# Label slots, first w7 loads, scaled tiles and early label rows moved in a one-core recommender kernel

## The reference, cut to what matters

```python
x: (1024, 50, 300)   label_embedding: (1024, 200, 300)      # all float32
q1 = attn_pool(x, mask, w1, b1, w2)      # softmax over 50 rows of exp((x @ w1 + b1) @ w2),
q2 = attn_pool(x, mask, w3, b3, w4)      # then the weighted sum of the rows
h = concat([q1, q2], axis=1) @ w5 + b5                      # (1024, 300)
f6 = h @ w6 + b6
iu, ju = triu_indices(300, k=1)                             # 44850 pairs
cross = h[:, iu] * h[:, ju] * (v @ v.T)[iu, ju]
f7 = cross @ w7 + b7                                        # (1024, 44850) @ (44850, 300)
out8 = concat([f6, f7], axis=1) @ w8 + b8                   # (1024, 300)
return einsum('bu,bku->bk', out8, label_embedding)          # (1024, 200)
```

## Time and profile before

| | |
|---|---|
| median of 3 runs | 1762.22 us (1760.65 to 1764.42) |
| time of the profiled execution | 1760.75 us |
| its span, first to last instruction | 1758.9 us |
| granted TensorE clock, mean | 0.968 |
| TensorE busy | 1583.0 us, 90% |
| VectorE busy | 1421.1 us, 81% |
| ScalarE busy | 996.4 us, 57% |
| DMA moved | 615.20 MB, mean 350 GB/s |

### The profile page before, as it was taken

The page is one execution under the profiler, slowest core; times in us unless marked ns, Lnnn a source line. Parts: engine busy times, 40 slices in busy tenths (PEclk is TensorE's granted clock), DMA queues, the critical chain, the costliest instruction groups (busy, mean ns, idle before and its releaser), DMA issues.

```text
span 1758.9 us, 25341 instructions
## 1 busy us (share of the span) xinstructions
PE 1583.0 (90%) x7086; PEld 1159.8 (66%) x7086; DVE 1421.1 (81%) x5487; ACT 996.4 (57%) x2931; POOL 137.9 (8%) x96
## 2 busy tenths in 40 slices
PE   2889999999999999999999999899999999998700
PEld 1467677677777777777777777577777777765400
DVE  8897888873898999799998986567777668678956
ACT  7665777764565646464655644344444444433497
POOL 5000000000000000000000000000000000003366
PEclk9999999999999999999999999899999999999955
DMA  7799877977899999999999899999999989999898
GB/s 295 268 390 369 288 273 242 330 279 258 299 332 388 364 409 354 413 357 370 392 359 395 324 393 383 413 358 328 359 381 374 334 314 406 350 357 406 329 397 361
DMA packets 170385, 615.20 MB, mean 350 GB/s; under 512 B 20784, under 2 KB 49421, under 8 KB 162053
## 3 DMA queue, kind: packets, MB, share of 16 engines
q1 hardware_dynamic: 106469, 368.44, 55.0%
q10 hardware_dynamic: 61696, 242.33, 37.0%
q0 software_dynamic: 2080, 2.81, 0.5%
HBM read 609.70 MB, written 3.79 MB: 349 GB/s over the span
## 4 chain that ended last, share of the span: by engine, by line
PE 66%; DMA 15%; DVE 11%; ACT 4%; issue 2%; POOL 1%; SPq 1%; ACTq 0%; DVEq 0%; POOLq 0%
PE bank L706 59%; DMA wring<-in_w7p 8%; DVE stream L1074 5%; DVE cring L1053 3%; DMA stream<-in_x 3%; PE bank L656 3%; DVE junk L953 2%; DMA stream<-in_label 2%; ACT stream L873 2%; PE bank L671 2%; DMA sring<-hrows 1%; ACT wring L862 1%; ACT stage L873 1%; PE bank L684 1%; ACT absjunk L771 1%
## 5 line engine op out<-in xcount | busy, mean ns | idle before, releaser
L706 PE MATMUL bank<-wring,cring 128*128 128x300 f32 (+1 forms) x5616 | 1445.3, 419 | 42.3 <-ACT wring L862 17.3
L706 PEld LDWEIGHTS bank<-wring,cring 128*128 128x128 f32 (+1 forms) x5616 | 1064.6, 191 | 407.2 <-issue 33.5
L862 ACT ACTIVATE wring<-wring,gcol 128x300 f32<-128x300 f32 x1403 | 655.4, 534 | 673.4 <-PE bank L706 579.9
L1053 DVE TENSOR_TENSOR cring<-lefts,sring 128x1024 f32<-128x1024 f32 (+2 forms) x312 | 372.5, 1194 | 190.5 <-PE bank L706 162.2
L1074 DVE SCALAR_TENSOR_TENSOR stream<-stream,out 128x300 f32<-128x300 f32 x1080 | 442.2, 469 | 0.0
L953 DVE SCALAR_TENSOR_TENSOR junk<-stream,ubc 128x300 bf16<-128x300 f32 x784 | 320.5, 469 | 28.3 <-DMA stream<-in_x 28.3
L771 ACT ACTIVATE absjunk<-stream 128x300 bf16<-128x300 f32 x448 | 196.0, 439 | 12.5 <-DMA stream<-in_x 7.1
L1074 DVE DVE_READ_ACCUMULATOR stream<-stream,out 128x1 f32 x1080 | 92.2, 85 | 0.0
L771 ACT ACTIVATION_READ_ACCUMULATOR absjunk<-stream 128x1 f32 x448 | 83.9, 187 | 0.0
L1074 DVE SCALAR_TENSOR_TENSOR stream<-stream,bank 128x300 f32<-128x300 f32 x160 | 64.8, 460 | 22.2 <-DMA stream<-in_label 22.2
L607 POOL DMA_DIRECT2D scores<-score x6 | 3.4, 570 | 987.8 <-DVE stream L1074 829.2
(11 more groups left out here) (94 smaller groups left out, 510.0 us busy)
## 6 DMA issues: line engine op xcount, KB each, us to landing
wring<-in_w7p ACTq DMA_DIRECT2D x365, 600.0 KB, 7.5
stream<-in_label SPq DMA_DIRECT2D x276, 750.0 KB, 10.4
stream<-in_x SPq DMA_DIRECT2D x64, 1050.0 KB, 12.6
sring<-hrows SPq DMA_DIRECT2D x152, 256.0 KB
stage<-in_label SPq DMA_DIRECT2D x44, 750.0 KB, 7.7
wring<-in_w7p ACTq DMA_DIRECT2D x18, 450.0 KB, 5.2
wring<-in_w7p ACTq DMA_DIRECT2D x18, 300.0 KB, 6.5
sring<-hrows SPq DMA_DIRECT2D x96, 44.0 KB
```

The source lines that it names most:

```text
L706: mm = pe.matmul(acc[b % 4][:, 0:E], cring[0:rows, p % CSLOTS, b % 2, j0 + j, :], w, start=(p == BEGIN[b] and j == 0), stop=(p == END[b] - ...
L862: ins = nc.scalar.activation(w, w, ACT.Copy, scale=gcol[:, t:t + 1])
L1053: nc.vector.tensor_tensor(cut(cring, p % CSLOTS, j0), in0, cut(sring, nb % SSLOTS, j0), ALU.mult).then_inc(c_ready, 1)
```

## The change

1. H_DONE, the step from which labels 139 to 142 may be loaded, is 258 in place of 248. Since the list of load steps never goes back and takes at most three labels in two steps, labels 139 to 161 and 163 move (139 to 141 to step 258, 142 to 144 to 260, and so on to 160 to 162 at 272); from 164 on to 240 nothing moves.
2. The first five w7 loads are issued by SyncE in its step -18, in its own queue behind the x loads, after waits for `g_ready` = 2 and `fold_out` = 3. ScalarE no longer waits or issues there.
3. From step 372 on `folded` is at most 1 in place of 2: ScalarE scales one tile more in each unit, VectorE folds one less.
4. EARLY_ROWS = 110 in place of 80. In steps 383 to 413 VectorE does 110 label rows of user tile 6; the tail has 58 labels in place of 64, and STOP is 472 in place of 478. FIRST_SHARED is 262.

```diff
-        return 0 if len(live(p)) == 2 or n == 1 else min(2, n - 1)
+        return 0 if len(live(p)) == 2 or n == 1 else min(1 if p >= END[-2] else 2, n - 1)
...
-    EARLY_ROWS = 80
+    EARLY_ROWS = 110
...
-    H_DONE = DOTS[NS - 1][1] + LATE[H_OUT] + 1
+    H_DONE = DOTS[NS - 1][1] + LATE[H_OUT] + 11
...
             for q in range(START, STOP):
+                if q == FIRST_W7:
+                    sp.wait_ge(g_ready, 2)
+                    sp.wait_ge(fold_out, NCH)
+                    for p in range(WSLOTS - 1):
+                        a, z = UNIT_TILE[p] * E, UNIT_TILE[p + 1] * E
+                        sp.dma_start(wring[:, p, 0:z - a], w7p[:, a:z]).then_inc(w7_in[p], 16)
...
-                if q == FIRST_W7:
-                    act.wait_ge(g_ready, 2)
-                    for p in range(WSLOTS - 1):
-                        w7_load(p)
```

## The result

| | before | after |
|---|---|---|
| median of the runs | 1761.43 us (6 runs, 1759.05 to 1764.42) | 1754.05 us (6 runs, 1753.03 to 1754.18) |
| ratio, 95% interval | | 0.9955 (0.9945 to 0.9966) |
| profiled execution, span | 1760.75, 1758.9 us | 1753.20, 1751.1 us |

The change makes the kernel 7.4 us or 0.45% faster. I had forecast 12.8 us less, with a range that holds the result. In the two traces the spans differ by 7.8 us, and this is made up of +3.7 before the w7 load of unit 264, -11.2 between the w7 loads of units 264 and 270, and -0.4 after it (each rounded by itself).

What follows compares the result with a forecast made beforehand. Bounds: a label queue stalling TensorE near 1100 us, TensorE from 1170 to 1550, then bytes over rate plus unused DMA time. Terms -11, -1.2 and -0.6 made -12.8, from median 1762.22 to 1749.4 us; range 1743 to 1758.

Steps and rivals of the forecast that it cites:

- rival B: Steps 260 to 280: label bursts delay a shifted-row load or SyncE stands on a full queue; 11.3 us per stall; chance 0.10.
- The first step: At the start: ScalarE is freed of 3.37 us of issues but needs the denominator, so only 0.3 to 0.4 us comes.
- freed of them it lands 2 to 3 us sooner: At the start: the store of h, without five w7 loads ahead in ScalarE's queue, lands 2 to 3 us sooner.
- the rule of the Trainium skill: Against part 2: moving DMAs to another engine gains only the sequencer's issue time; by it alone the term is -0.4.
- The comparison with GpSimd's store: At the start: h's store took 5.19 us on ScalarE's queue behind w7, one of the same size on GpSimd's 2.4 us.
- Rival C: Last stage gets worse: VectorE or labels slow w7 more than the tail gives back, +3 for -0.6, 1753; chance 0.12.
- unused 8.3 us: Between the one-user-tile stage and the tail: DMA unused until ScalarE's first tail sum frees a slot; 8.3 us, expected to stay.

Runs made afterwards that it cites:

- six labels ahead: Kernel before with H_DONE five steps later, so labels 139 to 144 stand ahead of the shifted-row load of step 256: 1752.22 us, ratio 0.9951.
- the changed kernel with early sums: Changed kernel with ScalarE's first four sums of the tail moved to steps 407, 409, 412 and 413: 1750.67 us, ratio 0.9935 to the kernel before.
- late slots with early sums: Kernel before with H_DONE ten steps later and ScalarE's first four tail sums moved from steps 414-419 to 407, 409, 412, 413: 1747.68 us, ratio 0.9937.
- x spread: Kernel before with the late label slots and the four x loads of a half tile, from step 53 on, spread over 2 steps each: 1751.58 us, ratio 0.9954.
- two w7 loads first: Late label slots and early tail sums, with ScalarE issuing two of the first five w7 loads at step -18, three at -1: 1750.40 us, ratio 0.9932.

## Why the prediction was right, and where its sizes were off

**Part 1, where the gain is.** The mechanism held at each point: the load of step 256 behind labels, the stall gone when they are moved, none in its place, and DMA time found between 1162 and 1542 us. The term was -11; alone it measured -9.0 (5.8 to 12.0 us). The mis-sized part is the removed stall, which I read from one execution. TensorE's gap there and the time between the w7 loads of units 264 and 270, in six traces of five programs that keep the labels early, and in those that don't:

| kernel | TensorE's gap near 1115 us | loads 264 to 270 |
|---|---|---|
| before | 8.6 | 32.8 us |
| w7 by SyncE alone | 4.7 | 29.3 |
| tile and rows | 7.1 | 30.4 |
| rows alone | 6.1 | 29.5 |
| tile alone, twice | 8.4 and 7.9 | 31.6 and 31.5 |
| the eight traces with labels later | 0 | 21.6 or 21.7 |

The six lose 11.2, 7.7, 8.8, 7.9, 10.0 and 9.9 us against 21.6, on average 9.2, close to the 9.0 measured. The trace shown happened to have the longest of them.

The queue after it was sized well enough, not exactly. I had the loads of shifted rows landing after 13 to 24 us; the labels among which they stand took 23.0 in the median. I had not foreseen that SyncE would stand on its own queue (9.89 us for five labels, 5.13 us for one pair of shifted rows), which I had put with rival B. It cost TensorE nothing: in that stretch it has no wait for VectorE. The kernel with six labels ahead shows how wide that margin is: 8.9 us of VectorE's waiting reached TensorE as nothing.

**Part 2, forecast -1.2, measured 0.0.** The time alone can't tell these two apart (within 2.5 us); the traces can. The first step was right: ScalarE's issues hid behind the denominator (4.07 us of waiting instead). The step that failed is "freed of them it lands 2 to 3 us sooner". It took 5.48 us with no w7 in its queue, and 5.22 us with this part alone. By the rule of the Trainium skill that I had set against it (page "DMA: Bandwidth & Descriptors", section "Issuing engines are not separate DMA queues") the term was -0.4, and the trace agrees with it better: the store was no faster, with this part alone the ratio was 1.0000, and without it alone 0.9956 against 0.9955.

In its place the runs show this. In 13 traces ScalarE's second store landed 0.35 to 0.45 us after the last of the five w7 loads, whichever engine had issued these and whether the store had been issued at 67.08 or at 71.36 us. With two loads ahead in place of five it landed 2.4 us sooner after its issue. The end of the bytes ahead sets it, and moving them to another queue does not move that end. More exactly it is the end of a small part of them. The semaphore of a DMA rises in 16 counts, as parts of it land. In the kernel before, 15 counts of the fifth w7 load had come by 71.60 us and the last came at 72.79; of the 32 counts of ScalarE's two stores, 30 had come by 72.03 and the last two at 73.05 and 73.22. One part in sixteen was late in both. The same page, section "Queues, rings and completion order", says that each raise of a DMA's semaphore lands only after every earlier write of the DMA engine that makes it, across its queues. The 13 landings agree with it.

The comparison with GpSimd's store, on which the forecast rested, was misread twice. The two stores are not of one size, as the issues from 60 to 76 us of the kernel before show for ScalarE's second one (compare):

```profile
hrows<-lefts ACTq DMA_DIRECT2D x1, 32.0 KB, 5.2
```

And its 2.4 us (landed at 72.21, before the fifth w7 load at 72.79) is not its own landing: four stores of GpSimd raise one semaphore, and 72.21 is its 16th count, whichever of the four had given it. The last of its 64 counts came at 73.93, after the w7 load. ScalarE's two stores share one too, but there the second landing is the 32nd count of 32, when both have landed.

**The first 264 units, forecast nothing, +3.7 us in the trace.** 1.1 us was lost before the moved loads: TensorE's first pooling was slower, and from 56 to 60 us the granted clock was down, as this stretch of the changed kernel shows:

```profile
56.00:60.00 4.00, 3.13 (x29) 1.46 (x32) 3.97 (x12) 2.61 (x12) 0.00 (x0) 0.60 0.94 384
```

The kernel before had 1.00 there and 64 records in place of 29. So the clock was at its lower level, 1.2 GHz, for most of it. TensorE had stood for 1.07 and 0.87 us just before, but so it had in the kernel before, without a dip. The kernel with w7 by SyncE alone has the same dip (0.62). The other kernel that moves these loads, the changed kernel with early sums, has 1.00 there and the dip from 62 to 69 us. And four kernels that do not move them have one between 62 and 70 us: the changed kernel with w7 given back, six labels ahead, late slots with early sums, and x spread. In six of these seven traces the first unit stands at 78.65 to 79.40 us, in the seventh, late slots with early sums, at 77.35; in the seven without a dip before 70 us it stands at 76.34 to 77.50. So the late first unit goes with the dip, whoever issues w7. Why the clock fell in these traces stays open. The rest are small stalls near 945 us, 3.2 us here and 1.1 before, which differ between all traces.

**Parts 3 and 4, forecast -0.6, measured 0.0 (0.9984 to 1.0016) together.** The sum is as it was put: the last unit 10.5 us later relative to step 372 (11.4 forecast), the tail 10.8 us shorter (11.2), -0.4 in all. That the small rest fits so well is luck: from step 372 to the end, five traces whose program there is that of before (the kernel before, labels later by five and ten steps, w7 by SyncE alone, x spread) take 224.9 to 228.7 us. DMA at 405 GB/s before and after. VectorE did not become the bound, though TensorE waited for it more often. Rival C had 0.12 and did not happen as a mechanism. Of the unused 8.3 us that I had named as what is left there, a good part was to be had by another edit, 5.9 us in the trace.

**The sum.** With the terms as measured, -9.0, 0.0 and 0.0 make -9.0 for the whole; the change measured -7.4, and without part 2 -7.9. The intervals of these (each about 2 to 3 us either way) overlap, so nothing more can be read from them. The result, 1754.05, lies 1 us above the band of my forecast (1744 to 1753) and in the one that I had given to rival C (1753 to 1755), whose mechanism did not happen. The number alone would have pointed to the wrong cause; the stated range held it because it was wide.

**The best version** by its median is the late slots with the early sums, 1747.68 us, ratio 0.9937 to the kernel before: it is below the changed kernel with one of its four parts and one edit that it does not have. The one with two w7 loads first measured 0.9932, the changed kernel with early sums 0.9935, and these three can't be told apart.

## What to carry to other kernels

A queue that holds both bulk loads and small urgent ones has to be read in program order: what stands ahead of the urgent load when it is issued, and how long until its user stands, counting every buffer between. Here moving the bulk behind it cost nothing, since later time was free to carry the bytes. In the stage where DMA was full, moving work earlier moved only its own bytes; the gain lay in the stretches where DMA was unused, and in the one event that ended each of them. And a stall read from one trace is one draw: size it from several executions, or give its term a range.

## What the hardware showed that I had not expected

The small stores issued while earlier loads were under way had both landed 0.35 to 0.45 us after the last of those loads, in 13 of 13 traces, also in the three where they were on another engine's queue than the loads. Both ends are set by a late sixteenth part: 15 of the 16 counts of the last load came 1.1 to 1.9 us before the sixteenth.

VectorE's 128x128 product of `lefts` and `sring` is held while GpSimd multiplies. Of the kernel before, GpSimd and VectorE in order of time:

```profile
1599.55 3.34 POOL L615 TENSOR_TENSOR stage<-stage,out 128x1500 f32<-128x1500 f32 x1 [12.57 <-DMA stage<-in_label]
```

```profile
1600.23 3.08 DVE L1036 SCALAR_TENSOR_TENSOR cring<-lefts,gcol,sring 128x128 f32<-128x128 f32 x2 [0.50 <-PE bank L706]
1607.13 0.61 DVE L1036 SCALAR_TENSOR_TENSOR cring<-lefts,gcol,sring 128x128 f32<-128x128 f32 x2 [0.70 <-PE bank L706]
```

Two of them took 3.08 us in that time and 0.61 us after it. It happened beside each of GpSimd's five products from 1580 to 1640 us, 1.26 to 3.08 us for the pair. Each time it is the first of the pair that is long, 1.00 to 2.82 us, and it ends 0.15 us after GpSimd's product, while the second takes 0.34 us. So it stands until GpSimd is done, and is not slowed by some factor. The label rows, whose second input is `bank` in PSUM, take 0.46 us beside GpSimd as elsewhere. The mean of 495 ns in the earlier trace rows, from which I had worked out what a folded tile costs, hides this: it is 0.3 us, or 1.0 to 2.8 us when it meets GpSimd. What the two engines contend for no run here shows.
